# Attention block of a post-norm MoE layer: four row tiles staged one step at a time instead of one tile end to end, and the weight-conversion loads cut to 256 KB on two buffers

## The reference

```python
x = layernorm(x + attention(x))    # 16 heads of 64, causal, softmax over up to 2048 keys
x = layernorm(x + moe(x))          # top-1 of 8 experts, weighted by the router's probability
# attention: q,k,v = x@Wq, x@Wk, x@Wv (+bias); scores = q@k.T/8, causal mask
#            pattern = softmax(scores); z = pattern@v; out = z@Wo + bo
# moe: for e in range(8): out += (sel == e)*wgt * (relu(x@w1[e] + b1[e]) @ w2[e] + b2[e])
```

## Time and profile before

| | us |
|---|---|
| median of 2 runs | 8157.06 (8114.06 and 8200.06) |
| the profiled execution, its own time | 8124.73 |
| its span, slowest core (core 0) | 8123.2 |
| span of the fastest core (core 5) | 8049.6 |

### The profile page before, as it was taken

One profiled execution on the slowest core, in us unless ns is written; L12 is line 12 of the kernel. 1 busy time (PEld: TensorE's weight loads), 2 busy tenths in 40 slices (PEclk: granted clock), 3 DMA queues, 4 the chain that ended last, 5 costly groups with the idle time before them and its releaser, 6 DMA issues. The chain is left out here.

```text
span 8123.2 us, 71081 instructions; the slowest of 8 cores (8049.6 to 8123.2 us)
## 1 busy us (share of the span) xinstructions
PE 5060.9 (62%) x21020; PEld 1927.0 (24%) x21370; DVE 1077.1 (13%) x1873; ACT 1684.0 (21%) x2518; POOL 212.1 (3%) x424
## 2 busy tenths in 40 slices
PE   4533444444433677777577777757777775777776
PEld 1111111111111222222222222222222222222222
DVE  0133333333322100000100000010000001000001
ACT  2134444444431111111111111111111111111111
POOL 0000110011000000000000000000000000000000
PEclk9855555555556799999899999989999998999999
DMA  2156656665664333333233333323333323333332
GB/s 66 39 113 132 126 125 123 135 126 125 134 134 111 92 104 106 108 104 104 75 103 109 108 103 104 92 92 109 103 100 108 106 83 97 103 104 105 108 103 77
DMA packets 583793, 852.14 MB, mean 105 GB/s; under 512 B 84472, under 2 KB 346888, under 8 KB 583440
## 3 DMA queue, kind: packets, MB, share of 16 engines
q1 hardware_dynamic: 380592, 444.81, 17.1%
q0 software_dynamic: 55392, 134.26, 11.5%
q10 hardware_dynamic: 147456, 268.50, 11.4%
HBM read 839.07 MB, written 142.61 MB: 121 GB/s over the span
## 5 line engine op out<-in xcount | busy, mean ns | idle before, releaser
L1026 PE MATMUL ps_all<-arena 128*128 128x512 bf16 x8032 | 1935.3, 381 | 827.3 <-DMA arena<-w2b 732.7
L990 PE MATMUL ps_all<-arena 128*128 128x512 bf16 x8024 | 1942.4, 382 | 465.8 <-PE ps_all L990 378.8
L1003 ACT ACTIVATE arena<-ps_all,arena 128x512 bf16<-128x512 f32 x1024 | 703.7, 687 | 4069.2 <-DMA arena<-w2b 2600.4
L1026 PEld LDWEIGHTS ps_all<-arena 128*128 128x128 bf16 x8192 | 730.6, 97 | 2030.8 <-issue 1324.9
L990 PEld LDWEIGHTS ps_all<-arena 128*128 128x128 bf16 x8192 | 732.5, 97 | 1678.0 <-issue 975.7
L1043 DVE SCALAR_TENSOR_TENSOR arena<-ps_all,arena 128x1024 f32<-128x1024 f32 x128 | 164.3, 1284 | 5024.1 <-PE ps_all L1026 5006.8
L507 PE MATMUL ps_sc<-arena 64*128 64x512 bf16 (+3 forms) x640 | 271.7, 546 | 630.5 <-ACT arena L525 596.8
L545 ACT ACTIVATE arena<-arena 128x128 bf16<-128x128 f32 (+15 forms) x256 | 307.5, 1201 | 418.1 <-DVE arena L531 291.8
L531 DVE TENSOR_REDUCE arena<-arena 128x1 f32<-128x128 f32 (+15 forms) x256 | 329.3, 1286 | 308.5 <-ACT arena L525 306.7
L576 PE MATMUL ps_ta<-arena 128*128 128x128 bf16 x1344 | 190.8, 282 | 285.5 <-ACT arena L588 167.6
L525 ACT COPY arena<-ps_sc 128x512 f32<-128x512 f32 (+5 forms) x240 | 243.0, 1012 | 366.7 <-DVE arena L519 366.7
(11 more groups left out here) (99 smaller groups left out, 1104.0 us busy)
## 6 DMA issues: line engine op xcount, KB each, us to landing
arena<-w1b SPq DMA_DIRECT2D x256, 1024.0 KB, 5.4
arena<-w2b ACTq DMA_DIRECT2D x1024, 256.0 KB, 2.6
arena<-w POOLq DMA_DIRECT2D x128, 512.0 KB, 6.3
w1b<-arena SPq DMA_DIRECT2D x128, 512.0 KB, 2.7
arena<-w POOLq DMA_DIRECT2D x256, 256.0 KB, 3.8
w2b<-arena SPq DMA_DIRECT2D x256, 256.0 KB, 2.0
arena<-x SPq DMA_DIRECT2D x32, 512.0 KB, 3.5
out<-arena SPq DMA_DIRECT2D x16, 512.0 KB, 2.6
```

The source lines that it names most:

```text
L990: ii = t.matmul(ps_all[:, b2_ * 512:(b2_ + 1) * 512], W1R[:, g2 % 4, dc, (f2 % 4) * 128:(f2 % 4 + 1) * 128], XT1[:, dc, :], start=(dc == 0 ...
L1003: return s.activation(HT[:, f2, :], ps_all[:, b2_ * 512:(b2_ + 1) * 512], AF.Relu, bias=b1s[:, e2, f2:f2 + 1], scale=1.0)
L1026: ii = t.matmul(ps_all[:, q * 1024 + half * 512: q * 1024 + (half + 1) * 512], HT[:, f2, q * 128:(q + 1) * 128], rhs[:, half * 512:(half + ...
```

## The change

Three things change in block 2.

1. The loop over the four tiles is cut into steps. All four `emit_scores` come first (without the maximum), then four `emit_max`, then `emit_av` of the head before, then four `emit_exp`, four `emit_norm`, and the transposes as before. Each tile has an f32 buffer (`P_sb_s`) and its own `smax`, `ssum` and `srr`. The copy of a tile also waits for the maximum of the same tile of the head before.
2. The four f32 buffers take the room of `cv_buf`. The conversion gets two buffers of 128 x 1024 bf16 in place of four of 128 x 2048, so load i waits for store i-2 rather than i-4.
3. The jobs of w1 are cut in two: 32 of 128 x 1024 for each expert in place of 16 of 128 x 2048. There are 512 jobs, all with 512 KB read and 256 KB written. The bytes in all stay the same.

```diff
-    P_sb = V(O_PSB, F32, 2048)
+    _PSZ = [1664, 1792, 1920, 2048]
+    P_sb_s = [V(D0 + 147456, F32, 1664), V(O_S1, F32, 1792),
+              V(O_STW, F32, 1920), V(O_STW2, F32, 2048)]
...
-    cv_buf = [V(O_STW, BF16, 2048), V(O_STW + 4096, BF16, 2048),
-              V(O_S1, BF16, 2048), V(O_S1 + 4096, BF16, 2048)]
+    cv_buf = [V(197312, BF16, 1024), V(199360, BF16, 1024)]
...
+            if fh > 0:
+                pg, ph = divmod(fh - 1, 16)
+                w_.append((cVE, mx_at[(pg, ph, s_)]))
...
-            for fh_ in range(2):
+            for fh_ in range(4):
                 cv_jobs.append((w1_h[e_, dc_ * 128:(dc_ + 1) * 128,
-                                     fh_ * 2048:(fh_ + 1) * 2048],
+                                     fh_ * 1024:(fh_ + 1) * 1024],
...
-        sl = i % 4
-        w = [(cCVO[sl], cv_out_at[i - 4])] if i >= 4 else []
+        sl = i % 2
+        w = [(cCVO[sl], cv_out_at[i - 2])] if i >= 2 else []
...
     for g, h in ghs:
-        emit_scores(g, h, 0)
-        emit_tail(g, h, 0)
-        for s_ in range(1, 4):
+        for s_ in range(4):
             emit_scores(g, h, s_)
-            emit_tail(g, h, s_)
+        for s_ in range(4):
+            emit_max(g, h, s_)
         if prev_av is not None and K_AV:
             emit_av(*prev_av)
+        for s_ in range(4):
+            emit_exp(g, h, s_)
+        for s_ in range(4):
+            emit_norm(g, h, s_)
         if K_TR:
             for s_ in range(4):
                 emit_transposes(g, h, s_)
```

More of the change, by code:

```diff
@@ L93, in build_nc @@
     ctx = ExitStack()
-    AR_BYTES = 204288
+    AR_BYTES = 204736
     ar = ctx.enter_context(nc.sbuf_tensor("arena", [128, AR_BYTES], mybir.dt.uint8))
@@ L138, in build_nc @@
     lrstd, lnmb, epsb, lm2, llog = SM(8), SM(9), SM(10), SM(11), SM(12)
+    smax_s = [SM(16 + i) for i in range(4)]
+    ssum_s = [SM(20 + i) for i in range(4)]
+    srr_s = [SM(24 + i) for i in range(4)]
     xstage = V(O_STX, F32, 2, 1024)
@@ L152, in build_nc @@
     ZT = V(O_ZT, BF16, 8, 2048)
-    P_bf_s = [V(O_STX, BF16, 2048), V(O_STX + 4096, BF16, 2048),
-              V(D0 + 147456, BF16, 2048), V(D0 + 151552, BF16, 2048)]
-    P_sb = V(O_PSB, F32, 2048)
+    _PSZ = [1664, 1792, 1920, 2048]
+    P_sb_s = [V(D0 + 147456, F32, 1664), V(O_S1, F32, 1792),
+              V(O_STW, F32, 1920), V(O_STW2, F32, 2048)]
+    P_bf_s = [V(201408, BF16, 1664), V(O_STXB, BF16, 1792),
+              V(O_STX + 4096, BF16, 1920), V(O_STX, BF16, 2048)]
     Wo_bf = V(O_WO, BF16, 8, 1024)
@@ L518, in emit_scores @@
         sfull = (4 * g + s_) * 128
-        sc.add("vector", (lambda sf: lambda v: v.tensor_add(
-            P_sb[0:128, sf:sf + 128], ps_sc[:, sf:sf + 128], madd[:, :]))(sfull),
+        psb = P_sb_s[s_]
+        sc.add("vector", (lambda sf, pb2: lambda v: v.tensor_add(
+            pb2[0:128, sf:sf + 128], ps_sc[:, sf:sf + 128], madd[:, :]))(sfull, psb),
             waits=[(cPE, scores_at[(g, h, s_)])], incs=[(cVE, 1)])
@@ L524, in emit_scores, with emit_max @@
         if sfull > 0:
[L525 to L528, removed]
-        evF_at[(g, h, s_)] = cSA.n
-        sc.add("vector", (lambda tu: lambda v: v.reduce_max(
-            smax[:, :], P_sb[0:128, 0:tu], AX.X, negate=True))(t_used),
+            w_ = [(cPE, scores_at[(g, h, s_)]), (cVE, evD_at[(g, h, s_)])]
+            pk = prev_key(g, h, s_) if s_ > 0 else None
+            fh = g * 16 + h
+            if fh > 0:
+                pg, ph = divmod(fh - 1, 16)
+                w_.append((cVE, mx_at[(pg, ph, s_)]))
+            sc.add("scalar", (lambda sf, pb2: lambda s: s.copy(
+                pb2[0:128, 0:sf], ps_sc[:, 0:sf]))(sfull, psb),
+                waits=w_, incs=[(cSA, 1)])
+        evF_at[(g, h, s_)] = cSA.n
+    def emit_max(g, h, s_):
+        t_used = (4 * g + s_ + 1) * 128
+        sc.add("vector", (lambda tu, s2: lambda v: v.reduce_max(
+            smax_s[s2][:, :], P_sb_s[s2][0:128, 0:tu], AX.X,
+            negate=True))(t_used, s_),
             waits=[(cSA, evF_at[(g, h, s_)]), (cVE, evD_at[(g, h, s_)])],
@@ L535, in emit_scores, with emit_exp @@
         mx_at[(g, h, s_)] = cVE.n
-    def emit_tail(g, h, s_):
+    def emit_exp(g, h, s_):
         t_used = (4 * g + s_ + 1) * 128
@@ L544, in emit_tail, with emit_norm @@
         pb = P_bf_s[s_]
-        sc.add("scalar", (lambda tu, pb2: lambda s: s.activation(
-            pb2[0:128, 0:tu], P_sb[0:128, 0:tu], AF.Exp,
-            bias=smax[:, 0:1], scale=1.0, accum_out=ssum[:, :]))(t_used, pb),
+        sc.add("scalar", (lambda tu, pb2, s2: lambda s: s.activation(
+            pb2[0:128, 0:tu], P_sb_s[s2][0:128, 0:tu], AF.Exp,
+            bias=smax_s[s2][:, 0:1], scale=1.0,
+            accum_out=ssum_s[s2][:, :]))(t_used, pb, s_),
             waits=w, incs=[(cSA, 1)])
         exp_at[(g, h, s_)] = cSA.n
[L551 to L554, removed]
+    def emit_norm(g, h, s_):
+        t_used = (4 * g + s_ + 1) * 128
+        pb = P_bf_s[s_]
+        sc.add("vector", (lambda s2: lambda v: v.reciprocal(
+            srr_s[s2][:, :], ssum_s[s2][:, :]))(s_),
+            waits=[(cSA, exp_at[(g, h, s_)])], incs=[(cVE, 1)])
+        sc.add("vector", (lambda tu, pb2, s2: lambda v: v.tensor_scalar_mul(
+            pb2[0:128, 0:tu], pb2[0:128, 0:tu], srr_s[s2][:, 0:1]))(t_used, pb, s_),
             incs=[(cVE, 1)])
@@ L640, in build_nc @@
         for dc_ in range(NDC):
-            for fh_ in range(2):
+            for fh_ in range(4):
                 cv_jobs.append((w1_h[e_, dc_ * 128:(dc_ + 1) * 128,
-                                     fh_ * 2048:(fh_ + 1) * 2048],
+                                     fh_ * 1024:(fh_ + 1) * 1024],
                                 w1b_h[e_, dc_ * 128:(dc_ + 1) * 128,
-                                      fh_ * 2048:(fh_ + 1) * 2048]))
+                                      fh_ * 1024:(fh_ + 1) * 1024]))
         for rc_ in range(FF // 128):
```

## The result

| | before | after |
|---|---|---|
| median | 8134.5 us (10 runs) | 8618.6 us (11 runs) |
| ratio, 95% interval | | 1.0585 (1.055 to 1.0621) |
| profiled execution, span of the slowest core | 8123.2 (core 0) | 8572.8 (core 2) |

Some executions of a kernel run with one die at a lower granted clock and take longer; the medians count them and the ratios leave them out. The changed kernel is 5.9% slower. The forecast had the direction, but 8385 us and a range up to 8470 were too low.

The account below looks back on a forecast made before the run. The conversion's chain of single loads was taken to bound block 2. Core 3, the slower: 8099.2 + 284 = 8383 us, plus 1.5 us of execution time over span, gave 8385 us (+2.8%), range 8300 to 8470.

Parts of the forecast that it names:

- What bounds the block: Block 2: the weight conversion's chain of single loads sets the end; attention has 148 us to spare on core 0.
- The number of gaps, the stops, the rest of the run: Conversion: 512 load gaps, four unexplained stops (27 us) instead of three; about 5590 us left after the first Wo load.
- The price of a narrow w1 load: Conversion: a halved w1 load costs 4.48 us like a w2 load, bounds 3.57 to 4.67; core 3 took 4.544.
- the forecast's chain: Conversion's 512 loads one after another: 2321.4 us on core 0, 2354.1 on core 3.
- Two buffers at no cost: Conversion: load i waiting for store i-2 adds 0 us; upper end +404 us.
- The order of attention, hidden: Block 2: attention runs under the conversion, so its new order saves nothing on the path.
- Its size: Attention in block 2: some 4 to 6 us shorter per group 3 head, ending perhaps 100 to 250 us earlier.
- the transposes: Attention head: transposes put at 4.7 + 7.9 = 12.6 us by the row of their copies.
- Too few buffers: Rival, conversion: stores hold up loads, gap goes to 4.8 us, time 8529 us; chance 0.08.
- the half price: Rival, conversion: a narrow w1 load costs 3.57 us, half a wide one, time about 8132 us; chance 0.04.
- The class "slower": Whole kernel: a measured time from 8320 us on counts as slower; chance 0.85.
- the nearest rival (8529): Rival, conversion: two buffers are too few, stores delay loads, +404 us; chance 0.08.

Follow-up runs that it names:

- conv_only: Kernel before with its old attention order and only the conversion changed (512 narrow loads, two buffers); ratio 1.0539.
- both_flat: Changed kernel with each narrow w1 job taken as 32 whole rows, pieces adjacent at source and target; 8479.0 us against 8239.8, ratio 1.0276.
- narrow_four: Kernel before with narrow w1 jobs at their old places, on four buffers; 8638.7 us against 8194.5.
- wide_two: Kernel before with its wide w1 jobs on two buffers; 8203.6 us.
- open_new_order: Changed kernel with adjacent w1 pieces, conversion queues no longer waiting for their own transfers; 8092.5 us, ratio 0.9857.
- mixed_new_order: open_new_order with exponentials, scalings and transposes taken in turn per tile, V product's copy after the second exponential; 8061.8 us.
- open_old_order: Kernel before with adjacent wide w1 jobs, four buffers, conversion queues not waiting for their own transfers; 8022.7 us, ratio 0.9775.
- old_wide_flat: Kernel before with only the wide w1 jobs' pieces made adjacent at source and target; 8178.3 us against 8193.6, ratio 0.9995.

## Why the prediction was right and wrong

- **What bounds the block: right.** The conversion sets the end, attention has slack, and what the conversion loses comes out one for one. conv_only shows the first two: 1.0539 with the old order, 1.0585 with the new, and the intervals overlap. The chain of loads grew by 454 us (2081 to 2535) and the span of the slowest core by 450, which shows the last.
- **The number of gaps, the stops, the rest of the run: right.** 512 loads, four stops, 28.5 us of them against the 27 taken, and 5588 us after Wo. The stops come 110 loads apart before and 112 apart after, not 128; that the number came out as four with either is luck. What they are stays open.
- **The price of a narrow w1 load: wrong, and this is the step that failed.** "I take 4.48, since a w2 load has the same 128 rows of 4 KB, the same queue and the same kind of target." Measured 5.29 to 5.38 us on the eight cores. On core 3, whose sum made the forecast, it is 5.36 us, 5.30 without the two stops that fell into w1; against the 4.54 taken that is 256 x 0.76 = +194 us. Its whole chain took 2549 us where 2354 were forecast, and the profiled execution lies 189 us above the forecast. The prediction had named the doubt ("The source rows of w1 lie 16 KB apart [...] which could cost a little") and then priced it at nothing. It gave 4.67 as the upper end, though the w2 parts, from which it came, all had adjacent pieces and so could not bound it. An upper end from its own rows was a whole wide load, 7.14 us. It also looked at the source alone: about half of the surplus is the store's. both_flat, in which this one thing is put right, lands on the forecast's chain and ratio.
- **Two buffers at no cost: right** while a queue waits for itself (narrow_four, wide_two, and no wait for a store in the changed kernel). Once it doesn't, they are the limit (open_new_order).
- **The order of attention, hidden: right. Its size: wrong.** Forecast 100 to 250 us earlier, measured about 32 (2351 against 2382 to 2384). The timeline of one head of group 3 in the changed kernel, TensorE first, then ScalarE:

```profile
2270.02 5.51 PE L639 MATMUL ps_zt<-arena 128*64 128x512 bf16 x16 [2.08 <-issue]
2279.45 0.38 PE L594 MATMUL ps_ta<-arena 128*128 128x128 bf16 x4 [3.93 <-DVE arena L571]
2280.36 0.38 PE L594 MATMUL ps_tb<-arena 128*128 128x128 bf16 x4 [0.52 <-PE ps_ta L594]
2285.62 0.58 PE L594 MATMUL ps_ta<-arena 128*128 128x128 bf16 x4 [4.88 <-ACT arena L606]
...
2298.44 1.54 PE L511 MATMUL ps_sc<-arena 64*128 64x512 bf16 x4 [0.36 <-PE ps_tb L594]
...
2275.62 0.58 ACT L647 CAST arena<-ps_zt 64x512 bf16<-64x512 f32 x1 [5.38 <-PE ps_zt L639]
2276.40 1.68 ACT L558 ACTIVATE arena<-arena 128x1664 bf16<-128x1664 f32 x1 [0.20 <-ACT arena L647]
...
2282.65 2.00 ACT L558 ACTIVATE arena<-arena 128x2048 bf16<-128x2048 f32 x1 [0.20 <-ACT arena L558]
...
2284.89 0.58 ACT L606 COPY arena<-ps_ta 128x512 bf16<-128x512 bf16 x1
```

and TensorE in the head of the earlier trace rows before:

```profile
2287.33 1.54 PE L507 MATMUL ps_sc<-arena 64*128 64x512 bf16 x4 [0.36 <-PE ps_tb L576]
...
2315.88 0.38 PE L576 MATMUL ps_ta<-arena 128*128 128x128 bf16 x4 [0.37 <-DVE arena L531]
...
2319.55 0.38 PE L576 MATMUL ps_ta<-arena 128*128 128x128 bf16 x4 [2.38 <-ACT arena L588]
...
2331.88 0.58 PE L507 MATMUL ps_sc<-arena 64*128 64x512 bf16 x1 [0.36 <-PE ps_tb L576]
```

This head starts at 2254.1 us. Up to its first transpose (scores, V product, first exponential and scaling) it takes 25.3 us, a little under the 26 to 28 forecast, where it took 28.6 before. TensorE then transposes two packs, and stops for 4.88 us: the copy that should empty its first pack stands on ScalarE behind the exponential of the fourth tile and starts at 2284.89. From the first transpose to the next head it is 19.0 us, before it was 16.0 (2315.88 to 2331.88). What was won ahead is lost there, and the head takes 44.3 us after 44.6. The term that failed is the transposes: they were put at 12.6 us by the row of ScalarE's copies alone, less than the 16.0 that they took even before, and side by side with the exponentials, without reading the order of ScalarE's list, where the copies come last. In mixed_new_order, where the copies stand between the exponentials, TensorE's longest stop among the transposes of its last head is 1.22 us, and they take 15.9 us from the first start to the last end, against 18.6 (core 5):

```profile
2177.20 0.59 PE L594 MATMUL ps_ta<-arena 128*128 128x128 bf16 x4 [3.13 <-DVE arena L571]
...
2183.42 0.58 PE L594 MATMUL ps_ta<-arena 128*128 128x128 bf16 x4 [1.22 <-ACT arena L606]
...
2192.53 0.59 PE L594 MATMUL ps_tb<-arena 128*128 128x128 bf16 x4 [0.36 <-PE ps_ta L594]
```

- **The rivals.** Too few buffers and the half price did not occur. The class "slower" was given 0.85 and came. The time lies above the forecast and above the nearest rival (8529), by a mechanism that had no rival of its own.

The Trainium skill has a rule that bears on the failed step. DMA: Bandwidth & Descriptors, section "Latency and other measured facts", says of copies between HBM tensors that a large power of two as the distance between the pieces of different partitions can halve the rate, and that laying the tiles out contiguously avoids it; it calls the mechanism, streams in step that hit the same HBM channels, an inference. Its distances start at 512 KB, where it still has nearly the full rate, so nothing in it foretells a cost at the 16 KB (source) and 8 KB (target) of this case. The runs agree with its remedy: narrow w1 gaps fall from 5.33 to 4.59 us with adjacent pieces. Why the same 16 KB does not hurt single transfers with pieces of 8 KB, and whether channels are the cause, no run here shows.

## What to carry to other kernels

The price of a transfer depends on its access pattern as well as on its size: before a DMA is cut, compare the length of its contiguous pieces and the distance between them on both sides with those of the DMA whose duration is borrowed. Where a chain of single transfers sets the end, cutting transfers multiplies their fixed part; the cure is to let the queue run ahead, and only then do buffers count. And before a reordering is priced, every engine's list has to be read to the end: here a copy behind four exponentials gave back most of what the new order had won.

## What the runs showed of the hardware

- One at a time, narrow w1 loads (4 KB pieces read 16 KB apart, 2 KB written 8 KB apart) came every 5.3 to 5.4 us, with adjacent pieces every 4.6; wide ones (8 KB read, 4 KB written) came every 6.8 to 7.3 us at the old places and every 7.0 to 7.2 with adjacent pieces.
- A store does not have to be waited for to cost: the same loads came every 5.33 us beside scattered stores and every 4.95 beside adjacent ones.
- Up to four transfers in flight move the same weights in 1332 to 1364 us (open_old_order) instead of 2081 to 2119 (old_wide_flat), while the single wide load takes longer to land (9.6 us on core 6, against 6.3 in the kernel before).
